# The attention's output projection as seven block products, and another order at the ends of the routed loops, of the logits' folding and of the last slots

## The reference

```python
x = x + 0.5 * ffn(layernorm(x), ...)
x = x + attn(layernorm(x), w_qkv, w_dense)
x = x + 0.5 * ffn(layernorm(x), ...)      # the same weights again

# attn: 32 query heads of 128 in 8 groups of 4, one key and value head per group
scores = where(causal, q @ k.T / sqrt(128), min);  o = softmax(scores) @ v
attn = concat(o over 32 heads) @ w_dense.T          # (1024 x 4096) @ (4096 x 512)
# ffn: a shared SiLU-gated part (512 inner) and 16 experts (128 inner), of which each token
#      takes its two likeliest, weighted
```

## Time and profile before

| | |
|---|---|
| median of 3 runs | 1143.31 us (1141.67 to 1143.67) |
| the profiled execution's own time | 1153.05 us |
| its span in the trace | 1151.2 us |
| granted TensorE clock, mean | 0.989 of 2.4 GHz |
| TensorE busy | 1107.8 us (96%) |
| VectorE, ScalarE, GpSimd busy | 58%, 49%, 41% |
| attention | about 197 to 960 us of the trace |

### The profile page before, as it was taken

How to read it: one execution, slowest core, us unless ns; L and a number is a source line. 1 busy time by engine, 2 the same in 40 slices (tenths; PEclk the granted TensorE clock), 3 DMA queues, 4 the chain that set the end, 5 groups by cost and what they waited for, 6 DMA issues and landing times.

```text
span 1151.2 us, 19600 instructions
## 1 busy us (share of the span) xinstructions
PE 1107.8 (96%) x6008; PEld 928.5 (81%) x6008; DVE 671.1 (58%) x1809; ACT 569.2 (49%) x1513; POOL 466.9 (41%) x484
## 2 busy tenths in 40 slices
PE   8889998899999999999999999999999999889996
PEld 6667877788888888888888888888888887667875
DVE  7668868754454545454545445454544557568866
ACT  4257753474455536446444545553553543257740
POOL 1546647154235325315323432522531420546643
PEclk9989999999999999999999999999999999999998
DMA  9995565001101100101010010110100006935555
GB/s 356 411 331 193 186 231 187 20 1 38 56 1 38 55 0 36 55 0 36 0 55 0 36 55 0 36 55 0 36 0 1 1 17 276 375 101 176 185 168 187
DMA packets 38617, 114.80 MB, mean 100 GB/s; under 512 B 4384, under 2 KB 4384, under 8 KB 36512
## 3 DMA queue, kind: packets, MB, share of 16 engines
q1 hardware_dynamic: 33440, 97.30, 23.3%
q0 software_dynamic: 5120, 16.78, 4.3%
HBM read 79.20 MB, written 34.87 MB: 99 GB/s over the span
## 4 chain that ended last, share of the span: by engine, by line
PE 83%; DVE 6%; ACT 3%; another core or an unknown queue 3%; issue 2%; DMA 2%; POOL 1%; SPq 0%; DVEq 0%; ACTq 0%; POOLq 0%
PE bank L1373 22%; PE bank L1405 15%; PE bank L1474 9%; PE bank L1434 9%; PE bank L1348 6%; PE bank L1386 6%; PE bank L1359 4%; PE bank L1262 4%; PE bank L1309 2%; DMA xn<-x_rows 1%; PE bank L1470 1%; PE bank L1430 1%; PE bank L1241 1%; PE bank L1281 1%
## 5 line engine op out<-in xcount | busy, mean ns | idle before, releaser
L537 POOL TENSOR_TENSOR scores<-scores,pinv 128x512 f32<-128x512 f32 (+3 forms) x256 | 176.7, 722 | 353.2 <-DVE pinv L1085 353.2
L480 POOL TENSOR_TENSOR tback_lo<-experts,tback_hi 128x768 fp32r<-128x768 f32 x62 | 114.3, 1846 | 83.2 <-ACT tback_hi L643 83.2
L705 ACT ACTIVATE pT_hi<-bank 128x512 fp32r<-128x512 f32 (+2 forms) x192 | 87.0, 488 | 112.4 <-PE bank L1386 112.4
L734 ACT ACTIVATE scores<-scores,nmax 128x512 f32<-128x512 f32 (+3 forms) x256 | 140.3, 558 | 0.0
L750 ACT ACTIVATE oT_hi<-bank 128x512 fp32r<-128x512 f32 x64 | 38.3, 599 | 204.3 <-PE bank L1470 204.3
L1059 DVE TENSOR_TENSOR pT_lo<-bank,pT_hi 128x512 fp32r<-128x512 f32 (+2 forms) x192 | 101.0, 554 | 52.7 <-ACT pT_hi L705 52.7
L1077 DVE CUSTOM_DVE_ANT_0 scores<-bank,causal 128x512 f32<-128x512 f32 (+3 forms) x256 | 112.3, 487 | 1.3 <-issue 0.3
L1063 DVE TENSOR_TENSOR oT_lo<-bank,oT_hi 128x512 fp32r<-128x512 f32 x64 | 44.3, 692 | 106.9 <-ACT oT_hi L750 106.9
L1373 PE MATMUL bank<-xnT_hi,wqs_hi 128*128 128x512 f32 x256 | 106.3, 415 | 0.0
L1405 PE MATMUL bank<-wds_hi,oT_hi 128*128 128x512 f32 x256 | 106.0, 414 | 0.0
L1373 PE MATMUL bank<-xnT_lo,wqs_hi 128*128 128x512 f32 x256 | 100.8, 394 | 0.0
(11 more groups left out here) (207 smaller groups left out, 2881.0 us busy)
## 6 DMA issues: line engine op xcount, KB each, us to landing
experts<-in_ffn_w SPq DMA_DIRECT2D x32, 768.0 KB
xn<-x_rows SPq DMA_DIRECT2D x62, 256.0 KB, 2.8
y_rows<-xn SPq DMA_DIRECT2D x62, 256.0 KB, 2.0
raw_q<-in_wq SPq DMA_DIRECT2D x8, 1024.0 KB
raw_d<-in_wd SPq DMA_DIRECT2D x8, 1024.0 KB
x_rows<-experts SPq DMA_DIRECT2D x1, 7936.0 KB, 30.0
raw_w<-in_ffn_w SPq DMA_DIRECT2D x8, 768.0 KB, 5.2
raw_kv<-in_wkv SPq DMA_DIRECT2D x8, 512.0 KB, 3.3
```

The source lines that it names most:

```text
L480: nc.gpsimd.tensor_tensor(tback[par][1][:], experts[:, bass.ds(at + FRONT, GU - FRONT)], tback[par][0][:].bitcast(F32), ALU.subtract).then ...
L537: nc.gpsimd.tensor_tensor(s, s, pinv[k % 2][:, i:i + 1].to_broadcast([P, P * (i + 1)]), ALU.mult).then_inc(att.normed, 1)
L705: nc.scalar.activation(pT[0][:, lo_col:hi_col], bank[b][:, 0:hi_col - lo_col], ACT.Copy).then_inc(att.t_hi, 1)
L734: nc.scalar.activation(s, s, ACT.Exp, bias=nmax[par][:, i:i + 1], scale=-1.0, accum_out=psumr[par][:, i:i + 1]).then_inc(att.exp, 1)
```

## The change

**The product.** A quad's product is (4 tiles x 4 heads) times (4 heads x 512 columns). The left side is cut in four blocks a11, a12, a21, a22 (two tiles by two heads each) and the right side in b11 to b22 (two heads by 256 columns). Seven block products in the form of Winograd replace the eight. The seven left operands (`PRODUCTS`) are a11, a12, a22 and the sums s1 to s4; the right ones are b11, b21, b22 and the differences t1 to t4 (`WEIGHT`). Each product is 2 tiles x 2 heads x 3 parts = 12 matmuls of 256 columns (L1616), 84 for a quad where 48 of 512 stood. All use bank 2 within the loop, one after the other: a product waits until VectorE has added the one before (`att.added`). A slot with k % 4 of 1, 2 or 3 holds two of them, the first right behind T01, the second behind T23; a slot with k % 4 = 0 holds s4 alone, behind T23.

**Its operands.** For each pair of heads ScalarE makes one copy of the first head (`first_o`, L825, 512 elements) and 7 high parts of 256 (L817), where two `oT_hi` of 512 stood; VectorE makes 7 low parts (L1224) and 4 sums (L1228), of 256 each, where two `oT_lo` of 512 stood. Three of the low parts and a sum come in the next slot, behind the masks and ahead of its `pT_lo`. For each group ScalarE makes 7 high parts of the right side (L809, 512 elements) for 4, GpSimd 7 low parts (L619) and 4 differences (L623), where 4 low parts stood. The differences t1 and then t2 and t4 are written over b11 in `raw_d`, t3 over b12, so each high part waits for its difference and the next difference for the low part.

**Elsewhere.** The products that fold the logits come behind a quarter of the first following `gate_up` half instead of at once. At the start of a routed loop one more tile of back weights is cut ahead of the loop, the cut of the next shared down weights moves behind it, and two of four `add_down` move behind the first hidden product. At its end, 12 products of a `gate_up` are put around the last `turn_hidden`, ahead of the last tile's down product; `combine(0)` moves behind the next two VectorE steps. More early tiles are taken before all experts are loaded (`EARLY_TILES`). At the end of the attention the last quad's seven products stand in the order `LAST` over banks 3, 0 and 2; `statistics(2, 0)` stands in VectorE's slot 64 ahead of that slot's `pT_lo`.

```diff
-EARLY_TILES = 7
+EARLY_TILES = 11
+PRODUCTS = ("a11", "s2", "s3", "a22", "a12", "s1", "s4")
+RIGHT = ("b11", "t3", "t1", "t2", "t4", "b21", "b22")
...
+                if k == 4:
+                    low("t1")
+                    combined("t2", "b22", "t1")
+                    low("t2")
...
+                    for i in {2: ("b11",), 3: ("t3",), 4: ("t1", "t2"), 5: ("t4",), 6: ("b21", "b22")}.get(k, ()):
+                        right_hi(g, i)
...
+                def right_hi(g, i):
+                    if i == "b11":
                         act.wait_ge(loaded.d, 16 * (g + 1))
+                    if i in ("t1", "t2", "t3", "t4"):
+                        act.wait_ge(att.right_sum, 4 * g + ("t1", "t3", "t2", "t4").index(i) + 1)
...
-                            nc.scalar.activation(oT[bu][ru][0][:], bank[1][:], ACT.Copy).then_inc(att.pv_hi, 1)
+                        heads(g, k)
...
+                    late = r in (1, 3) and exists(u, 3, UNITS + 1)
+                    if isinstance(u, int) and u == UNITS:
+                        add_product(products(g, k)[-1], b=0)
+                        norm_then = statistics(2, 0)
+                    if late:
+                        for i, src in (("s3", o_diff[:]), ("s1", first_o[:, 2 * P:]), ("s2", first_o[:, 0:2 * P])):
+                            left_lo(g, k - 1, i, src)
+                        left_sum(first_o[:, 0:2 * P], bank[1][:, 0:2 * P], first_o[:, 0:2 * P], ALU.subtract)
...
+                    pe.wait_ge(att.right_lo, NP * (quad // 2 if isinstance(quad, int) else g - (k < 5)) + n + 1)
+                    pe.wait_ge(att.left_lo, 2 * NP * quad + NP + LEFT.index(i) + 1)
...
+                    elif not isinstance(before, int) or o_bank is bank[2] or i == "s4":
+                        wait(pe, att.added, before)
+                    for half in range(2):
+                        m = 0
+                        for head_pair in range(2):
                             for a, z in PARTS:
-                                last = nc.tensor.matmul(o_bank(u)[:], oT[ob][h][a][:, tile * P:(tile + 1) * P],
-                                                        wds[h][z][:], start=(m == 0), stop=(m == 3 * G - 1))
+                                last = nc.tensor.matmul(o_bank[:, half * 2 * P:(half + 1) * 2 * P],
+                                                        left(i, head_pair, b)[a][:, half * P:(half + 1) * P],
+                                                        right[WEIGHT[i]][z][:, head_pair], start=(fresh and half + m == 0),
...
-                gate_up(n, 1)
+                gate_up(n, 1, (1,), range(0, 1))
+                fold_logits(n)
+                gate_up(n, 1, (0,))
+                gate_up(n, 1, (1,), range(1, 2))
+                rank(n)
+                gate_up(n, 1, (1,), range(2, HC))
```

More of the change, by code:

```diff
@@ L265, in att_tail, with products, quad_of, left @@
                 slot(KV - 1, k)
-        def o_bank(u):
-            return bank[(0, 1, 2, 3)[u - UNITS - 1] if isinstance(u, int) and u > UNITS else 2]
         UNITS = KV * BATCH * G
+        def products(g, k):
+            u = 8 * g + k
+            if isinstance(u, int) and u > UNITS:
+                done = NP * (2 * KV - 1)
+                if u == UNITS + 1:
+                    return [(i, done + LAST.index(i), bank[LAST_BANK[i]]) for i in LAST]
+                return []
+            if not exists(u, 5, UNITS):
+                return []
+            first = 2 * ((k - 5) % 4)
+            done = 2 * NP * (g + k // 8) + DONE[k % 8]
+            return [(i, done + n, bank[0 if isinstance(u, int) and u >= UNITS - 1 and i in ("s1", "s4") else 2])
+                    for n, i in enumerate(PRODUCTS[first:first + 2])]
+        def quad_of(g, k):
+            return 2 * g + (k - 5) // 4
+        def left(i, head_pair, b):
+            return left1[i] if head_pair else left0[b][i]
+        def last_read(i, g, k, head_pair):
+            quad = 2 * g + (k - 1) // 4
+            b = (k - 1) // 4 % 2
+            back = 1 if head_pair or left0[0][i] is left0[1][i] else 2
+            return NP * (quad - back) + PRODUCTS.index(i) + 1
+        def evacuated(g, k):
+            quad, r = 2 * g + k // 4, k % 4
+            if r == 0:
+                return att.left_lo, 2 * NP * (quad - 1) + NP + 1
+            if r == 1:
+                return att.left_sum, 2 * len(SUMS) * quad
+            if r == 2:
+                return att.left_lo, 2 * NP * quad + 1
+            return att.left_sum, 2 * len(SUMS) * quad + len(SUMS)
         PROJ_AHEAD = 4
@@ L292, in cuts @@
             flat = "p c d -> p (c d)"
[L293 to L297 removed]
+            base = 6 + 6 * g
             if exists(8 * g + k, 0, UNITS - 9):
@@ L1063, in low, with add_product @@
                     nc.vector.tensor_tensor(dst, src, hi.bitcast(F32), ALU.subtract).then_inc(s, 1)
+                def add_product(product, b):
+                    i, before, o_bank = product
+                    half, c = BLOCK[i]
+                    part = x[:, 4 * b + 2 * half:4 * b + 2 * half + 2, c * (HID // 2):(c + 1) * (HID // 2)]
+                    dve.wait_ge(att.o_mm, before + 1)
+                    if isinstance(before, int) and before >= NP * (2 * KV - 1):
+                        for p in [p for p in LAST[:LAST.index(i)] if BLOCK[p] == BLOCK[i]][-1:]:
+                            dve.wait_ge(att.added, NP * (2 * KV - 1) + LAST.index(p) + 1)
+                    nc.vector.tensor_tensor(part, o_bank[:].rearrange("p (t c) -> p t c", t=2), part,
+                                            ALU.add).then_inc(att.added, 1)
@@ L1237, in first_gate_up @@
                         if n == 1 and m == 0:
-                            pe.wait_ge(att.added, UNITS - 3 + 2 * half)
+                            if half == 0:
+                                pe.wait_ge(att.added, NP * (2 * KV - 1) + LAST.index("a12") + 1)
+                            else:
+                                pe.wait_ge(att.added, NP * (2 * KV - 1) + LAST.index("s4") + 1)
                         for c in range(HC):
@@ L1436, in slot @@
                             last.then_inc(att.s_mm, 1)
+                    todo = products(g, k)
+                    if isinstance(u, int) and u == UNITS:
+                        dense(todo.pop(), g, k)
                     if exists(u, 1, UNITS):
```

317 lines of the change are left out of this document (219 added, 98 removed).

## The result

The changed kernel takes 1162.81 us (median of 4 runs, 1161.06 to 1164.97) against 1143.49 (4 runs, 1141.67 to 1145.42). The ratio is 1.0169, 95% interval 1.0148 to 1.0189: 19.3 us slower. The forecast was 1150, in a range from 1135 to 1161. The direction was right and the size three times too small: 6.5 us were forecast.

The account below looks back on a forecast made before the run. TensorE was taken as the bound in the attention loop. -15.8 + 16.8 + 3.2 + 4 - 2.3 = +5.9 us, carried over to the median 1143.31, gave 1149.2, set to 1150 for likelier contention; range 1135 to 1161.

Parts of the forecast that it names:

- The products: Attention's output projection: 84 matmuls of 256 columns per quad instead of 48 of 512, -15.8 us over 16 quads.
- The wait in slot 5: Attention groups: TensorE waits 1.1 ahead of T23 and 0.9 at the second product; 2.1 taken, eight times, +16.8 us.
- ScalarE's six-link chain: Slots 4 and 5: sums, copies and t2's difference on three engines delay the first `pT_hi` to 6.65 from 3.38.
- the contention: VectorE operations with two SBUF inputs wait for GpSimd; slot 5's wait becomes 2.35 instead of 2.0 if it falls there.
- The shorter waits: Attention outside slot 5: low parts and sums delay TensorE 0.4 us per group, eight groups, +3.2 (1.6 to 5.6).
- The last slots: Attention slots 63 and 64: waits for low parts, an add and the statistics, net +4 us (+1 to +6).
- The ends: Routed loops' start and end, folding and tile loads, outside the attention: together -2.3 us.
- The start's gain: Start of a routed loop: 1.4 of TensorE's 1.94 wait for `tfront_lo` goes, twice, -2.8 us (-3.8 to -1.5).
- the late row: End of a routed loop: last down product, row DMA and gathers start 2.0 us later each; net +2.0 (-1.6 to +4).
- contention as the rule: Odd slots: VectorE and GpSimd collide, TensorE waits 1 us in two more slots per group, +16, 1166 us; chance 0.08.

Follow-up runs that it names:

- e2: Changed kernel with t1 cut in slot 3 and t2's difference made first in GpSimd's slot 4; 1153.7 us, ratio 1.0100 to the kernel before.
- e4: Changed kernel with the edits of e2 and e3 together; 1137.9 us, ratio 0.9965 to the kernel before.
- e5: Changed kernel with ten matmuls of 256 columns, read by nobody, ahead of T23 in slot 5; 1152.8 us, ratio 1.0111 to the kernel before.
- e3: Changed kernel with low parts of s3 and s1 moved behind the softmax's on VectorE in odd slots; 1161.8 us, ratio 1.0171 to the kernel before.

## Why the prediction was right or wrong

1. *The products, -15.8: right.* I added the distances from start to start of all matmuls of one group, by line. The products take 22.74 us before and 21.08 after, 1.66 less. The projections, without the pause behind one of them, take 34.51 and 34.13, 0.38 less: the first fp32r matmul behind a fp32 transpose costs 0.08 more, and now it is more often a product that pays. Together -2.04 per group where -1.98 was forecast, -16.3 in all.
2. *The wait in slot 5, +16.8: right in place and nearly in size, half right in its cause.* The prediction split 2.1 into 1.1 and 0.9, and the brackets say 1.39 and 0.51. From start to start the last projection matmul and T23 are 1.78 apart for 0.24, and T23's last transpose and the second product 0.79 for 0.03: 2.30 lost per group, 2.12 in the first and 1.70 in the last, 17.6 in all. But its text made ScalarE's six-link chain the cause and priced the contention at 0.35 inside it. e2 shows that VectorE's low parts behind GpSimd are a full second cause.
3. *The shorter waits, +3.2: half as much.* The period is 0.47 longer than before; without the products (-2.04) and slot 5 (+2.30) 0.21 is left, 1.7 in eight groups, at the low end of the range. In the two full-clock groups whose matmuls I went through, no pause shows outside slot 5. Part of the reason may be a wrong count: the prediction has GpSimd do 15 operations of 1.27 per group for 4, and it is 11 for 4.
4. *The last slots, +4: right.* By the brackets 6.3 for 1.5, +4.8.
5. *The step that failed: in the term of +16.8 I had a pause cost its own length and nothing more.* The sum of points 1 to 4 is +8.2 as predicted and, with what was measured for each, -16.3 + 17.6 + 1.7 + 4.8 = +7.8. The attention lost 18.5. The clock makes the difference, 9.5 in the trace: 6.1 in four groups of 1.53, and 3.4 in the last slots, where PV took 2.54 and the 36 matmuls behind it 7.03, against 1.81 and 4.39 in e4, which keeps its clock there. 7.8 + 9.5 = 17.3 of the 18.5. e5 takes back the 6.1 of the groups, with all their waits in place. In the trace of before the half clock had begun in pauses of 6.7, 5.3 and 3.8 us, and full clock stood behind 1.94 and 2.50. I took that as licence to price 1.1 and 0.9 at their length; the prediction has no term and no rival for it. I had overlooked a place in that same trace:

```profile
973.10 1.06 PE L1220 MATMUL bank<-fold,wide 32*128 32x16 f32 x8 [0.69 <-ACT wide L577]
...
975.71 0.63 PE L1262 MATMUL bank<-xnT_hi,wgu_lo 128*128 128x512 f32 x1
```

The granted clock is at half from 975.36 to 978.77, behind this pause of 0.69 and sixteen products of 16 columns. So a short pause could be followed by half clock, and the forecast had reason for a rival on it.

6. *The ends, -2.3: wrong, 0.* The start's gain is real in its row, but a wait for a tile's rows takes most of it, and nothing of it is left at the attention's first scores; the price of 2.0 a pass for the late row is refuted.
7. 1150 + 9.5 for the clock + 2.3 for the ends is 1161.8, and 1162.8 was measured.

Of the rivals, contention as the rule (1166) had the right size by the wrong price: it asked for two more waits of 1 us a group, and there are none.

What stays open: why 1.39 + 0.51 drop the clock in one group and not in the next, with the same instructions and the same distances between them, and why 1.73 in one piece, in the old kernel, doesn't. The half clock doesn't begin at a fixed place behind the pause: 0.64, 0.20, 0.86 and 0.45 us behind the second product's start in the four groups of the changed kernel, and from 0.1 ahead of it to 0.8 behind it in e3. It wasn't tried to vary the two pauses and the gap between them by themselves.

## What to carry to other kernels

Look for all chains that end at the same wait before you price one of them or take it away: here two ended 0.8 us apart; undoing one gave less than half of the loss, undoing the other nothing, and both together all of it and more. Where TensorE is the bound, a pause can cost twice, by its length and by the clock behind it. Look in the trace of before for half clock behind short pauses too, outside the stretch that the change touches. A way to tell whether a pause has this second cost is to fill it with matmuls that nobody reads and time the kernel. And operations that were moved to 256 elements with both inputs in SBUF stop being cheap when GpSimd is given more to do in the same slots: put those that nobody awaits behind the ones that the next matmul waits for.
